# Later blocks' x loaded as whole rows and turned by TensorE and VectorE, in place of 128-byte pieces turned by VectorE alone

## Time and profile before

| | us |
|---|---|
| median of 3 runs | 2768.39 |
| lowest, highest | 2765.13, 2770.02 |
| the profiled execution's own time | 2765.76 |
| its span in the trace | 2764.1 |

### The profile page before, as it was taken

The page is one execution under the profiler, slowest core; times in us unless marked ns, Lnnn a source line. Parts: engine busy times, 40 slices in busy tenths (PEclk is TensorE's granted clock), DMA queues, the critical chain, the costliest instruction groups (busy, mean ns, idle before and its releaser), DMA issues.

```text
span 2764.1 us, 22872 instructions
## 1 busy us (share of the span) xinstructions
PE 2748.6 (99%) x7043; PEld 1283.4 (46%) x7043; DVE 2419.4 (88%) x2563; ACT 892.2 (32%) x674; POOL 54.4 (2%) x113
## 2 busy tenths in 40 slices
PE   9999999999999999999999999999999999999998
PEld 6444444444444444444554444444444444444455
DVE  6888888888888888888899898989898989898988
ACT  5555555555555555555541000001010101010101
POOL 0000000000000000000000000000000000000000
PEclk9999999999999999999999999999999999999999
DMA  9999999999999999999880000000000101010000
GB/s 307 356 315 311 309 319 311 314 315 311 318 313 315 314 312 316 315 314 317 254 217 1 19 18 17 21 14 25 10 28 6 31 3 34 0 34 0 16 0 21
DMA packets 292907, 468.13 MB, mean 169 GB/s; under 512 B 17339, under 2 KB 124974, under 8 KB 292718
## 3 DMA queue, kind: packets, MB, share of 16 engines
q1 hardware_dynamic: 156062, 233.88, 28.3%
q10 hardware_dynamic: 134224, 228.67, 26.0%
q0 software_dynamic: 2560, 4.86, 0.6%
HBM read 443.79 MB, written 23.55 MB: 169 GB/s over the span
## 4 chain that ended last, share of the span: by engine, by line
PE 97%; DVE 2%; ACT 0%; DMA 0%; issue 0%; ACTq 0%; SPq 0%; DVEq 0%
PE bank L587 48%; PE bank L628 24%; PE bank L633 23%; PE bank L561 1%; PE bank L585 1%; PE bank L616 1%; DVE adj_t L951 0%; DVE adj_t L684 0%; PE bank L500 0%; PE bank L656 0%; DVE area_h L846 0%; DMA area_h<-in_L_gnn_item_feat_dram 0%; ACT area_p L1058 0%; PE bank L491 0%; ACTq L314 0%
## 5 line engine op out<-in xcount | busy, mean ns | idle before, releaser
L587 PE MATMUL bank<-adj_t,area_h 128*128 128x512 f32 (+1 forms) x3160 | 1334.3, 582 | 0.7 <-DVE adj_t L684 0.7
L951 DVE SCALAR_TENSOR_TENSOR adj_t<-area_r,c_col,area_h 128x1024 f32<-128x1024 uint8 (+2 forms) x782 | 948.7, 1257 | 117.2 <-PE bank L633 115.9
L684 DVE STREAM_TRANSPOSE adj_t<-area_r 128x2048 f32<-128x2048 f32 (+3 forms) x400 | 893.0, 2233 | 172.4 <-PE bank L587 104.5
L587 PEld LDWEIGHTS bank<-adj_t,area_h 128*128 128x128 f32 x3160 | 597.0, 190 | 713.0 <-issue 705.8
L1068 ACT ACTIVATE mask_out<-adj_t 128x4096 uint8<-128x4096 f32 (+1 forms) x200 | 700.1, 3501 | 643.3 <-DVE packing L762 362.3
L628 PE MATMUL bank<-adj_t,area_r 128*128 128x512 f32 x1564 | 797.9, 592 | 1.2 <-DVE adj_t L951 1.2
L633 PE MATMUL bank<-adj_t,area_r 128*128 128x512 f32 (+1 forms) x1548 | 765.3, 576 | 0.0
L633 PEld LDWEIGHTS bank<-adj_t,area_r 128*128 128x128 f32 x1548 | 294.1, 190 | 370.2 <-issue 370.2
L628 PEld LDWEIGHTS bank<-adj_t,area_r 128*128 128x128 f32 x1564 | 296.1, 190 | 346.3 <-issue 326.7
L846 DVE TENSOR_TENSOR area_h<-area_p,bit_of 128x2048 uint32<-128x2048 uint32 (+4 forms) x101 | 220.9, 2188 | 0.0
L1195 ACT ACTIVATE area_h<-bank,empty_sums 128x512 f32<-128x512 f32 x9 | 6.2, 687 | 431.2 <-PE bank L633 431.2
(11 more groups left out here) (143 smaller groups left out, 494.1 us busy)
## 6 DMA issues: line engine op xcount, KB each, us to landing
area_r<-in_adj_dram SPq DMA_DIRECT2D x312, 512.0 KB, 9.6
area_r<-in_adj_dram ACTq DMA_DIRECT2D x312, 512.0 KB, 10.0
area_r<-in_adj_dram SPq DMA_DIRECT2D x78, 480.0 KB, 8.7
area_r<-in_adj_dram ACTq DMA_DIRECT2D x78, 480.0 KB, 8.9
mask_scratch<-packed ACTq DMA_DIRECT2D x40, 320.0 KB, 7.8
area_p<-mask_scratch SPq DMA_DIRECT2D x20, 640.0 KB, 6.1
x_scratch<-area_s ACTq DMA_DIRECT2D x20, 256.0 KB, 5.7
area_h<-x_scratch SPq DMA_DIRECT2D x10, 512.0 KB, 3.9
```

The source lines that it names most:

```text
L587: mm = nc.tensor.matmul(acc1[par][:, 0:live], h[:, c * SPC + s, :], adj_t[:, c % 2, s * width:s * width + live], start=(c == 0 and s == 0) ...
L684: nc.vector.transpose(dst, src).then_inc(half_turned, 1)
L951: nc.vector.scalar_tensor_tensor(out=prob_of(k, b)[:, 0:width], in0=lhs, scalar=c_col[:, b:b + 1], in1=unpacked[:, c % 2, n, 0:width // 4] ...
```

## The change

`load_x` becomes one DMA per block, from POOL as before, of whole rows: four nodes (2048 bytes) to each of 128 partitions (68 in the last block). Four transposes on PE behind chunk 2 of every later block, ahead of `z_rows`, turn it into bank 1 of PSUM; they wait for `x_loaded` and for `x_turned` of the block before. DVE's `x_transposed` becomes the copy that block 0 has had, waiting for the new semaphore `x_rows_turned`. POOL's wait for `x_turned` becomes one for `x_rows_turned`. In block 0 the transposes go to bank 1 as well, and wait for `weights_turned_sb`.

```diff
--- before.py
+++ after.py
@@ -150,6 +150,7 @@
         acc1 = (banks[5], banks[0])
         ps_z, ps_tst = banks[3:5], banks[2]
         ps_weights = banks[0:2]
+        ps_x = banks[1]
         item_banks = (banks[4:6], banks[2:4])
         h_banks = (banks[0:2], banks[6:8])
         ps_setup = banks[6:8]
@@ -170,7 +171,7 @@
         vectors_loaded = sem("vectors_loaded")
         vectors_spread = sem("vectors_spread")
         vectors_sb = sem("vectors_sb")
-        first_x_turned = sem("first_x_turned")
+        x_rows_turned = sem("x_rows_turned")
         w_item_turned = sem("w_item_turned")
         w_item_turned_sb = sem("w_item_turned_sb")
         item_turned = sem("item_turned")
@@ -329,22 +330,13 @@
                     rows = rows.rearrange("(s j) d -> j s d", j=Q)
                 eng.dma_start(home, rows).then_inc(item_loaded[group], 16)
 
-        def load_x(eng, k, width, quarters):
-
-            eng.wait_ge(x_turned, k)
+        def load_x(eng, k, width):
+
+            eng.wait_ge(x_rows_turned, k)
             eng.wait_ge(half_turned, (k - 1) * HALVES + 2 * 6)
-            blocks_in = x_in.rearrange("p (b f) -> p b f", f=Q)
-            for a in quarters:
-                cols = slice(a * Q, (a + 1) * Q)
-                if width == IB:
-                    src = x[bass.ds(k * IB, IB), cols].rearrange("(b i) f -> i b f", i=Q)
-                    eng.dma_start(blocks_in[a * Q:(a + 1) * Q, :, :], src).then_inc(x_loaded, 16)
-                else:
-                    full = TAIL // Q
-                    src = x[NB * IB:NB * IB + full * Q, cols].rearrange("(b i) f -> i b f", i=Q)
-                    eng.dma_start(blocks_in[a * Q:(a + 1) * Q, 0:full, :], src).then_inc(x_loaded, 16)
-                    rest = TAIL - full * Q
-                    eng.dma_start(blocks_in[a * Q:a * Q + rest, full, :], x[N - rest:N, cols]).then_inc(x_loaded, 16)
+            rows = x[bass.ds(k * IB, IB), :] if width == IB else x[NB * IB:N, :]
+            live = P if width == IB else TAIL // TPB
+            eng.dma_start(x_in[0:live, :], rows.rearrange("(p t) d -> p (t d)", t=TPB)).then_inc(x_loaded, 16)
 
         @block.sync
         def _(sp):
@@ -471,7 +463,7 @@
 
             def x_loads(k, par, width, first):
                 if not first:
-                    load_x(pool, k, IB if width == IB else TW, range(A))
+                    load_x(pool, k, width)
 
             blocks(pool, x_loads)
 
@@ -529,6 +521,11 @@
                     pe.wait_ge(vectors_sb, 1)
                 h_products(c)
 
+            def x_transposes(k, live):
+                for t in range(TPB):
+                    mm = nc.tensor.transpose(ps_x[:, t * P:t * P + live], x_in[0:live, t * D:(t + 1) * D], ident[0:live, 0:live])
+                mm.then_inc(x_rows_turned, 1)
+
             def weight_products(c):
 
                 if c == 4:
@@ -539,9 +536,8 @@
                     mm.then_inc(weights_turned, 1)
                 if c == 5:
                     pe.wait_ge(first_x_loaded, 16)
-                    for t in range(TPB):
-                        mm = nc.tensor.transpose(banks[2][:, t * P:(t + 1) * P], x_in[:, t * D:(t + 1) * D], ident)
-                    mm.then_inc(first_x_turned, 1)
+                    pe.wait_ge(weights_turned_sb, 1)
+                    x_transposes(0, P)
                 if c == 6:
                     pe.wait_ge(weights_turned_sb, 1)
                     nc.tensor.matmul(banks[3][:, 0:2], w_t[:, 2, :], a_cols[:, :], start=True, stop=True).then_inc(wa_product, 1)
@@ -592,6 +588,9 @@
                         weight_products(c)
                     else:
                         if c == 2:
+                            pe.wait_ge(x_loaded, 16 * k)
+                            pe.wait_ge(x_turned, k)
+                            x_transposes(k, P if width == IB else TAIL // TPB)
                             z_rows(k - 1, IB)
                         if c == 7:
                             scores_back(k - 1)
@@ -688,14 +687,12 @@
                 nc.vector.tensor_tensor(yz[:, 0:width], yz[:, 0:width], x_t[:, 0:width], ALU.add).then_inc(residual_added, 1)
 
             def x_transposed(k, width):
-                if is_first(k):
-                    dve.wait_ge(first_x_turned, 1)
-                    nc.vector.tensor_copy(x_t.rearrange("p (i t) -> p i t", t=TPB),
-                                      banks[2][:, :].rearrange("p (t i) -> p i t", t=TPB)).then_inc(x_turned, 1)
-                    return
-                dve.wait_ge(x_loaded, (0 if width == IB else 64) + 64 * k)
-                dve.wait_ge(residual_added, k)
-                nc.vector.transpose(x_t[:, 0:width], x_in[:, 0:width]).then_inc(x_turned, 1)
+                live = P if width == IB else TAIL // TPB
+                dve.wait_ge(x_rows_turned, k + 1)
+                if not is_first(k):
+                    dve.wait_ge(residual_added, k)
+                nc.vector.tensor_copy(x_t[:, 0:TPB * live].rearrange("p (i t) -> p i t", t=TPB),
+                                      ps_x[:, :].rearrange("p (t i) -> p i t", t=TPB)[:, 0:live, :]).then_inc(x_turned, 1)
 
             def z_of(t):
                 return ps_z[t // 2], (t % 2) * TZ
```

## The result

The changed kernel takes 2774.54 us, the median of 9 runs (2773.05 to 2778.03), against 2768.39 us before. The ratio is 1.0028, with a 95% interval from 1.0018 to 1.0039: slower by 0.28%, some 7.8 us. 2776.8 us and 0.30% had been forecast.

A forecast was written before the change was run, and what follows sets the result against it. PE's own work was taken to bound layer 1. 7.9 us for transposes in 18 full blocks plus 0.5 us in the last block made 8.4 us slower, a median of 2776.8 us, range 2771 to 2785 us.

The forecast's parts named there:

- What bounds the kernel: Layer 1: PE's own work sets the pace; work added there is paid in full, relief of DVE, POOL or DMA brings nothing.
- The four transposes: PE, behind chunk 2 of each later block: 0.44 us for four, as in block 0; 7.9 us for 18 full blocks.
- The other bound: PE's four transposes, each waiting for the last one's end: 4 x 0.272 = 1.09 us a block.
- DVE's lag: Full blocks: DVE's copy waits for PE, chunk 4's first half starts 1.1 us later; no cost, 2.2 us of cover remain.
- The last block: Last block of layer 1, where the chain runs through DVE: 0.5 us slower, with 0.2 and 0.8 as ends.
- the two figures I had: Last block: DVE's copy starts some 0.4 to 0.64 us later than the transpose of x did.
- PE's new waits: PE's transposes wait for x landed and x_turned; x is issued some 56 us before PE asks for it: no cost.
- The sum: Whole kernel: 7.9 + 0.5 = 8.4 us slower, forecast median 2776.8 us, 0.30% more.
- DMA sets the pace: Rival, layer 1: DMA traffic stretches PE's reading, whole rows give time back; 2768 us or a little below, chance 0.10.
- Transposes in series: Rival, PE: 1.09 us for four transposes, 20.7 us in all, 2789 us; chance 0.05.
- DVE's lag as a cost in the full blocks: Rival: DVE's lag reaches PE at chunk 4, 18 x 1.1 = 20 us more, 2797 us; chance 0.05.
- a late x: Rival: x lands late, needing a landing nine times as long; each microsecond from there costs 19; chance 0.02.

The follow-up runs named there:

- experiment 1: Kernel before, plus four unneeded transposes on PE behind chunk 2 of every later block, no wait added: 2776.5 us, ratio 1.0029.
- experiment 3: Changed kernel with each of the four transposes of a later block done twice, eight in a row: 2784.8 us, ratio 1.0059 to the kernel before.
- experiment 2: Changed kernel without its transposes on PE: whole rows in one DMA, DVE's transpose as before, x not fully turned: 2768.23 us, ratio 0.9999.
- experiment 4: Changed kernel with the four transposes behind chunk 1 in place of chunk 2: 2776.76 us, ratio 1.0030 to the kernel before.
- experiment 6: Changed kernel with DVE's copy of a later block done three times, two of them to unused PSUM banks: 2775.13 us, ratio 1.0030 to the kernel before.
- experiment 5: Changed kernel with the four transposes behind chunk 3 in place of chunk 2, DVE's copy where it was: 2929.87 us, ratio 1.0584.
- experiment 7: Kernel before with twelve more matmuls of ones at the start, where PE waits for DMA: 2765.57 us, ratio 0.9991.
- experiment 8: Changed kernel with twelve more matmuls of ones at the start: 2774.12 us, ratio 1.0023 to the kernel before.

## Why the prediction was right

**What bounds the kernel** held: PE's own work sets the pace of layer 1, and what was put on it was paid in full (experiments 1 and 3), while what was taken off DMA and POOL brought nothing (experiment 2). DVE's work was the same before and after, so nothing here shows what relief of DVE would bring.

**The four transposes** were priced at 0.44 us from one place in block 0, and cost 0.44 us in each of the 18 full blocks. The other bound, the records' 0.272 us each, fell: four starts lie 0.11 us apart here too, although z_rows follows. With it fell the reading of the figure in "TensorE: Matmul & The Clock Gate" of the Trainium skill, section "Part 4: PE-mode transpose", about 275 ns, as a cost in a chain: the records last that long (0.273 us), and eight in a row cost 0.87 us. The section names bf16, and the transposes here are float32.

**DVE's lag** was put at 1.1 us and at no cost in the full blocks. It was 0.99: chunk 4's first half began 204.35 - 203.10 = 1.25 us after PE was through with chunk 2, before 199.80 - 199.54 = 0.26, by the timelines. PE's lines there, first before, then after:

```profile
199.54 1.06 PE L561 MATMUL bank<-z_right,area_s 128*128 128x130 f32 x8
...
203.10 0.60 PE L526 MATMUL bank<-z_right,area_s 128*128 128x128 f32 x4
```

Chunk 4's second half was done at 206.88 + 2.30 = 209.18, and PE came to chunk 4 at 204.60 + 6.87 = 211.47 by the chain: 2.3 us of cover were left, where I had put 2.2. Experiments 4 and 6 show from both sides that it was free, and experiment 5 that it would not have been with a chunk less of cover.

**The last block** was put at 0.5 us, between 0.2 and 0.8, and took 0.38: 0.16 for PE's transposes (experiment 1's stretch, 7.64 - 17 x 0.44) and 0.22 for DVE's wait. The parts carry the rounding of 17 times 0.44, some 0.1 us at most. Its copy began, by the timelines, at 1385.83, 0.45 us after the first of the transposes, near the lower of the two figures I had:

```profile
1385.38 0.41 PE L526 MATMUL bank<-z_right,area_s 68*128 68x68 f32 x4
```

**PE's new waits** cost nothing: x still lands some 50 us before it is needed (issued at 217.03 us in block 2, landed 6.9 us later, and wanted at 273.4).

**The sum** was 8.4 us. The traces give 8.30 within the span. Another 0.4 us, for which the sum had no term, lies around it: 2.05 us of the profiled execution, 1.66 before. In all runs whose span is on record it goes with the load in one DMA (1.95 to 2.08 us in the kernels that have it, experiment 2 among them, and 1.57 to 1.70 in the others); its cause was not looked for. Together that is 8.7, and experiments 7 and 8 say 8.55, the start's difference included. The median of the changed kernel came out 2.3 us under the forecast because of the start. Six of the nine runs of before lie in its upper group, from 2768.32 us on, and so does their median; of the changed kernel's nine, five lie in the lower one, the median among them. Group against group the means differ by 8.2 and 8.8 us. So how near the medians came to the forecast was the luck of how many runs fell into each group: the chain bears the sum out, the medians alone would not. I had carried the forecast over to the median with 2.6 us of that spread, and had taken it for noise without asking where it lies.

The rivals fell one by one. That DMA sets the pace, experiment 2 excludes to some 2.8 us by the lower end of its interval and to 0.01 us by the chain. Transposes in series are excluded by the 0.109 us each of experiment 3, DVE's lag as a cost in the full blocks by experiments 4 to 6, and a late x by the landing after 6.9 us.

## What to carry to other kernels

Where one engine runs without a gap, the price of moving work to it can be read from a single place where it already does that work, by the step between starts in the chain and not by the records' durations; and relief elsewhere is worth nothing until somebody on the chain waits for it. A new wait on another engine is free as long as the lag is less than the cover behind it, which is to be counted up to the instant at which the bound engine wants the result. Where a change is worth 0.3%, look for the stretch of the kernel in which its runs differ from each other, before timing anything.

## What was not expected

- A gap of 5.5 us on PE cost half as much again: the granted clock fell from 1.00 to 0.50 within it, and the 16 records behind it took 9.74 us in place of 6.87 (experiment 5).
- Some 3 us of the kernel's run-to-run spread lie ahead of layer 1, in its first 40 us. Twelve matmuls that compute nothing narrowed the kernel before to 1.4 us between its lowest and highest run and took its median from 2768.4 to 2765.6 us (experiment 7). That the clock is the whole cause is not shown: in the changed kernel's own profile the eight transposes of the second chunk of items took 1.97 us, against 1.09 before, in a stretch whose row grants 1.00.
- 2560 packets became 1504 for the same 4.86 MB, at the same share of the DMA engines: in the records the 128-byte pieces were packets of 1.9 KB on average.
